# Where the tiles of an attention kernel begin in SBUF, by 256 bytes, and the step between the chunks of its turned x

## The reference, cut to what matters

```python
xn = _layernorm(x)
c_Q, c_KV = xn @ W_DQ.T, xn @ W_DKV.T                  # latents, 128 wide
q = concat(c_Q @ W_UQ.T, rope(c_Q @ W_QR.T))           # 16 heads, 128 + 64
k = concat(c_KV @ W_UK.T, rope(xn @ W_KR.T))           # the 64 are shared by the heads
v = c_KV @ W_UV.T
s = softmax(causal(clip(q @ k.T, -80, 80)) / sqrt(192)) @ v @ W_O.T
g = silu(xn @ weight.T + mixture of 8 rank-16 experts, top 2)
out = x + s * g
```

## Time and profile before

| | |
|---|---|
| median of 3 runs | 1417.05 us (1416.91 to 1419.74) |
| the profiled execution | 1419.24 us, its span 1417.7 us |
| PE busy | 1381.3 us, 97% of the span |
| DVE busy | 1144.5 us, 81% |
| ACT busy | 781.9 us, 55% |
| mean granted TensorE clock | 0.995 of full speed |

### The profile page before, as it was taken

How to read it: one execution, slowest core, us unless ns; L and a number is a source line. 1 busy time by engine, 2 the same in 40 slices (tenths; PEclk the granted TensorE clock), 3 DMA queues, 4 the chain that set the end, 5 groups by cost and what they waited for, 6 DMA issues and landing times.

```text
span 1417.7 us, 27675 instructions
## 1 busy us (share of the span) xinstructions
PE 1381.3 (97%) x9810; PEld 1156.7 (82%) x9810; DVE 1144.5 (81%) x1339; ACT 781.9 (55%) x861; POOL 125.7 (9%) x175
## 2 busy tenths in 40 slices
PE   7999689999999999999999999999999999999998
PEld 6888568778788888888888889888899688878887
DVE  7666378898898898989889898898788888967664
ACT  4232357666666666666666666666656656533221
POOL 0000111201101101010010100111100011012221
PEclk9999899999999999999999999999999999999999
DMA  7332664545435333334242432444412233166552
GB/s 291 118 100 79 193 199 150 173 138 150 122 96 149 107 108 85 120 87 126 63 122 85 104 110 63 118 153 140 134 56 61 69 109 115 49 197 173 174 159 89
DMA packets 110769, 174.91 MB, mean 123 GB/s; under 512 B 9608, under 2 KB 65160, under 8 KB 108168
## 3 DMA queue, kind: packets, MB, share of 16 engines
q1 hardware_dynamic: 93880, 108.99, 24.6%
q0 software_dynamic: 16016, 63.80, 15.4%
q10 hardware_dynamic: 832, 1.57, 0.5%
HBM read 125.83 MB, written 48.50 MB: 123 GB/s over the span
## 4 chain that ended last, share of the span: by engine, by line
PE 72%; DVE 9%; ACT 3%; DMA 2%; issue 2%; POOL 0%; SPq 0%; DVEq 0%; ACTq 0%; POOLq 0%
PE score_ps L1244 29%; PE out_ps L1266 19%; PE score_ps L1363 3%; PE score_ps L1365 3%; PE score_ps L1364 3%; DVE prob_l L1560 3%; ACT prob_h L1423 2%; DVE prob L1547 1%; DVE prod L1519 1%; PE out_ps L1285 1%; PE out_ps L1289 1%; PE out_ps L1286 1%; DVE total L1555 1%; PE score_ps L1214 1%; PE score_ps L1215 1%
## 5 line engine op out<-in xcount | busy, mean ns | idle before, releaser
L1423 ACT CAST prob_h<-prob 128x1024 fp32r<-128x1024 f32 (+1 forms) x288 | 289.6, 1006 | 237.3 <-DVE prob L1542 189.6
L1560 DVE TENSOR_TENSOR prob_l<-prob,prob_h 128x1024 fp32r<-128x1024 f32 (+1 forms) x288 | 336.0, 1167 | 39.6 <-ACT prob_h L1423 38.2
L1244 PE MATMUL score_ps<-q_h,key_slot 64*128 64x512 f32 x1792 | 365.8, 390 | 0.0
L1417 ACT ACTIVATE prob<-score_ps 128x1024 f32<-128x1024 f32 (+1 forms) x288 | 281.9, 979 | 145.8 <-PE score_ps L1244 96.5
L1266 PE MATMUL out_ps<-prob_h,value_slot 64*128 64x512 f32 (+1 forms) x1792 | 351.9, 378 | 0.7
L1555 DVE TENSOR_TENSOR total<-total,prob 128x1024 f32<-128x1024 f32 (+1 forms) x256 | 294.9, 1152 | 0.0
L1542 DVE TENSOR_SCALAR prob<-prob 128x1024 f32<-128x1024 f32 x224 | 155.1, 692 | 70.4 <-ACT prob L1417 70.1
L1266 PEld LDWEIGHTS out_ps<-prob_h,value_slot 64*128 64x128 f32 x1792 | 180.8, 184 | 35.5 <-DVE prob_l L1560 6.8
L1244 PEld LDWEIGHTS score_ps<-q_h,key_slot 64*128 64x128 f32 x1792 | 180.8, 184 | 28.1 <-issue 5.1
L1244 PE MATMUL score_ps<-rot_hh,key_slot 64*128 64x512 f32 x896 | 181.8, 388 | 0.0
L1244 PE MATMUL score_ps<-q_l,key_slot 64*128 64x512 f32 x896 | 181.6, 387 | 0.0
(11 more groups left out here) (210 smaller groups left out, 2005.2 us busy)
## 6 DMA issues: line engine op xcount, KB each, us to landing
key_slot<-keys SPq DMA_DIRECT2D x144, 256.0 KB, 2.6
value_slot<-values SPq DMA_DIRECT2D x144, 128.0 KB, 2.3
rot_hh<-turned POOLq DMA_DIRECT2D x30, 512.0 KB, 6.3
heads_rows<-head_rows POOLq DMA_DIRECT2D x15, 1024.0 KB, 9.7
turned<-rot_hl POOLq DMA_DIRECT2D x14, 1024.0 KB, 5.2
rows<-heads_rows SPq DMA_DIRECT2D x28, 512.0 KB, 5.7
rot_l<-turned POOLq DMA_DIRECT2D x30, 256.0 KB, 7.6
x_in<-in_x SPq DMA_DIRECT2D x16, 256.0 KB, 2.7
```

The source lines that it names most:

```text
L1244: mm = pe.matmul(score_ps[:, half, c * 512:(c + 1) * 512], keys_of[ROWS[r], :], moving[par][ROWS[r], half * HW + c * 512:half * HW + (c + ...
L1417: nc.scalar.activation(prob[half][:, 0:width], score_ps[:, half, 0:width], ACT.Exp, scale=QK_SCALE).then_inc(exp_done, 1)
L1423: nc.scalar.copy(prob_h[half][:, 0:width], prob[half][:, 0:width]).then_inc(high_done, 1)
L1560: nc.vector.tensor_tensor(p_l, p, p_h, ALU.subtract).then_inc(split, 1)
```

## The change

`ones`, 32 words of 128 bytes, is moved from the end of the persistent tiles to their start, so all others of them begin 128 bytes higher; what comes behind them stays where it was. `edge`, the tile at the right end, grows from 24 to 56 words, so every tile of Top begins 128 bytes lower. In prepare `small` (2176 bytes, 128 more than a multiple of 256) is moved between w_h and w_l. The chunks of xt_h and xt_l are 520 words apart instead of 512 (CHUNK_STEP is 1032 % 64, so 8 words), of which 512 are used, and three tiles of 128 bytes (rt0, rt1, rt2) are moved ahead of, between and behind them. No instruction is added or taken away, and none changes its number of columns.

```diff
+CHUNK_STEP = C_ALL % 64
-EDGE = 24
+EDGE = 56
@@ Persistent
+        self.ones = sb("ones", [P, 32], F32)
         ((self.cos, self.sin, self.qr_h, self.qr_l), (self.wo_first,),
...
         self.causal = sb("causal", [P, CT], F32)
-        self.ones = sb("ones", [P, 32], F32)
@@ prepare
         w_h = sb("w_h", [P, KC, C_ALL], F32R)
+        small = sb("small", [P, GROUP, ER + EXPERTS])
         w_l = sb("w_l", [P, KC, C_ALL], F32R)
+        rt = [sb("rt0", [P, GROUP, EXPERTS])]
+        xt_h = sb("xt_h", [P, KC, GT + CHUNK_STEP], F32R)
+        rt.append(sb("rt1", [P, GROUP, EXPERTS]))
+        xt_l = sb("xt_l", [P, KC, GT + CHUNK_STEP], F32R)
+        rt.append(sb("rt2", [P, GROUP, EXPERTS]))
         xn = sb("xn", [P, GROUP, DIM])
...
-        xt_h = sb("xt_h", [P, KC, GT], F32R)
-        xt_l = sb("xt_l", [P, KC, GT], F32R)
...
-        small = sb("small", [P, GROUP, ER + EXPERTS])
...
-        rt = [sb(f"rt{n}", [P, GROUP, EXPERTS]) for n in range(5)]
+        rt += [sb(f"rt{n}", [P, GROUP, EXPERTS]) for n in (3, 4)]
@@ prepare, PE, L377
-            ... ws[:, c, col:col + P], xs[:, c, :],
+            ... ws[:, c, col:col + P], xs[:, c, 0:GT],
```

More of the change, by code:

```diff
@@ L376, in group @@
                         for ws, xs in ((w_h, xt_h), (w_l, xt_h), (w_h, xt_l)):
-                            mm = pe.matmul(work_ps[:, (GROUP + k) % 2, :], ws[:, c, col:col + P], xs[:, c, :],
+                            mm = pe.matmul(work_ps[:, (GROUP + k) % 2, :], ws[:, c, col:col + P], xs[:, c, 0:GT],
                                            start=(n == 0), stop=(n == 3 * KC - 1))
```

## The result

The changed kernel takes 1410.28 us in the median of 4 runs (1408.36 to 1410.77), against 1418.17 us for the kernel before (1416.91 to 1419.74): a ratio of 0.9941, 95% interval 0.9925 to 0.9957. The forecast was 1408.9 us, with a range from 1406 to 1413.5; it was counted from 1417.05 us, the median of the kernel before at that time, and the same 8.2 us taken from 1418.17 would give 1410.0. Run again later (e11) the changed kernel gave 0.9948 (0.9934 to 0.9961).

The account below looks back on a forecast made before the run. PE, busy 97% of the span, was taken as the bound. Terms of 4.6 + 0.6 + 1.8 + 1.2 = 8.2 us, taken from the median 1417.05, gave 1408.9 us, range 1406 to 1413.5.

Parts of the forecast that it names:

- Full stretches of par 0: Attention's full tiles on par 0 buffers become as fast as par 1's: 4.6 us won, bounds 3.5 and 5.5.
- The 9.2 us named beside it: Gain in par 0's full stretches if a full 5.5 ns came on 56 x 30 pairs; not the figure taken.
- Corner and late tiles: Par 0's units between full stretches, 0.12 us shorter five times, none at the DVE-bound start: 0.6 us, bounds 0.3 and 1.2.
- Projection: Par 1's projection tiles go from 10.92 to 10.66 us, seven of eight counted: 1.8 us, bounds 1.5 and 2.1.
- prepare: Matmuls of L406, L417 to L419 and partly L377 get faster, less waits: 1.2 us won, bounds 0 and 2.3.
- the sign named for it: In prepare, L406 comes down to 227 to 229 ns a matmul if the forecast is right.
- The guess for L377: In prepare, its 144 matmuls stay 32 bytes apart; gain between nothing and 6.6 ns each (0.95 us), 0.3 us taken.
- No effect: Rival: the par difference hangs on something the change leaves, such as buffer distance; time stays at 1417 us; chance 0.08.
- The bound moves: Rival: ACT, DVE or stores wait instead, in prepare and projection; half the gain given back, about 1413 us; chance 0.13.
- Slower by the 520-word step: Rival: ACT's and DVE's writes of xt (L459, L575) slow down; 15.3 us if doubled, 1424 us; chance 0.03.

Follow-up runs that it names:

- e11: The changed kernel itself, run again beside e12: 1411.14 us, 0.9948 of the kernel before.
- e6: Against the changed kernel, chunks of w_h and w_l 1088 words apart and xt's 512, all beginning at remainder 128: 1410.02 us, 0.9944 of the kernel before.
- e8: Against the changed kernel, xt's chunks 512 words apart again instead of 520: 1411.97 us, a single run.
- e7: As e6, with the weight columns reordered so every slice a matmul reads begins at remainder 128: 1410.33 us, 0.9944 of the kernel before.
- e12: e7 run again, beside e11: 1409.98 us, 0.9940 of the kernel before.
- e2: Only prepare's tiles moved as in the change, attention's operands left as in the kernel before: 1417.23 us, 0.9997 of the kernel before.
- e3: The changed kernel with edge at 40 words instead of 56, so Top at remainder 64: 1422.53 us, a single run.
- e4: The changed kernel with edge at 48 words instead of 56, so Top at remainder 32: 1421.75 us, a single run.

## Why the prediction was right, point by point

*Full stretches of par 0*, 4.6 us with bounds 3.5 and 5.5: 5.0 in par 0's own, 0.4 given back in par 1's, so 4.6. The step that carried it, reading par 1's stretch as what par 0's would become, held to a hundredth of a us for eight tiles: 54.31 forecast, 54.31 measured. For fourteen it was 0.3 us short (1.44 read, 96.19 - 94.44 = 1.75 measured), in part because par 1's stretch has the wait of its own that is shown above. The 9.2 us named beside it count the pairs of L1266 as apart, which they are not by the addresses.

*Corner and late tiles*, 0.6: 1.0. The five ways into later stretches of par 0 are 0.12 to 0.13 shorter each, as read. The remaining 0.37 is at the one after the second stretch (18.92 to 18.55), which only gives back the 0.34 that this stretch lost (12.98 to 13.32); the two together are unchanged, as forecast for the units that DVE bounds.

*Projection*, 1.8: 2.1, eight tiles of par 1 at 0.19 to 0.28. Leaving out one of them because of the wait behind it was wrong, since in the other profiles the same place costs between 0 and 0.5 us. A stall that is seen in one profile was taken as part of the kernel.

*prepare*, 1.2 with bounds 0 and 2.3: this is the term that was mis-sized. The sentence that failed is "192 matmuls of L406 get stationary and moving operands of one rest; only from chunk to chunk the rest steps by 32 ... At 5.5 ns this is 1.3 us". The step was taken as harmless, and it spoils most of the gain: L406 won 0.7 to 0.9 ns instead of 5.5, and the sign named for it, 227 to 229 ns, did not come. e6 shows it by removing the step from all four operands, 231.3 to 227.9 ns, while e8, which removes it from xt alone, makes L406 slower. The guess for L377, between nothing and 6.6 ns, came out near 1 ns (232.8 to 231.8), and e7 shows that its 32 bytes cost most of the difference (227.9 without them). From the second group to the fourth the changed kernel won 0.2 us (62.13 to 61.93) and e12 0.9 (61.24), and e2 is 0.9997 of before.

The sum, 8.2 us, against 7.9 in the medians. By the starts the four terms measured 4.6, 1.0, 2.1 and 0.1, which is 7.8: about 1 us too much in prepare and 0.7 too little at the ways and the projection nearly cancel. The mechanism and its place were forecast; that the total came out so near is in part luck.

*The rivals.* No effect, with the place in SBUF as the cause: fell with the first result, and e3 and e4, where Top moves by 32 and 64 bytes and par 0 is slow again, settle it. What spoke for it, the Trainium skill's page "SBUF — State Buffer", section "A bandwidth-pool intuition that's wrong (but worth ruling out)", gives PE's weight loads a second independent read port. The runs here do not agree with the reading that the two streams cannot touch each other: one word between their rests costs 1.8 to 2.1 us on 420 pairs, some 4 to 5 ns each, and so does the changed kernel's edge moved by 32 bytes (e4, 94.44 to 96.50 us). The bound moves: not seen, from the second pair on par 0's stretches are within 0.04 us of par 1's, the longest is shorter, and PE's share of the chain rose. Slower by the 520-word step: the writes are at 586 and 691 ns as before.

## What to carry to other kernels

In a stream of fp32r matmuls of 512 columns with a weight load each, let every stationary and moving operand begin at the same remainder by 256 bytes, chunk steps and column offsets included: 226.6 ns a matmul against 231 to 233. Of the remainders 0, 32 and 128 each was fast when shared; every difference that was tried, from 4 to 128 bytes, cost most or all of the price; and one odd operand in three brings up the mean of the whole stream. Where a kernel keeps a buffer twice, compare the two copies' stretches in its own trace before changing anything.

## What was not expected of the hardware

The price does not grow with the difference: fourteen full tiles take 94.44 us at a distance of 0, and 96.55, 96.62, 96.50, 96.64 and 96.19 us at 4, 16, 32, 64 and 128 bytes, so the largest difference is the cheapest. It lasts for some matmuls after a break (e7: five distances of 228 to 236 ns, then 226 and 227). It is not clearly seen in shorter matmuls: L365, 264 columns, takes 122 to 123 ns before, after and in e7. That the period is 256 bytes and not more follows from the tile of par 0 of the kernel before, where rows_h0 (16512) and merged_l (186240) are 663 x 256 bytes apart, an odd multiple, and the distance is 226.8 ns. That it is not 128 or a smaller power of two follows from those distances costing too. The mechanism stays open: that the weight load and the running matmul meet in reading SBUF fits all of this, but no run shows the two reads.
